# Result rows scattered to their token by GpSimd, and read back with plain loads

## The reference

```python
x = x + 0.5 * ffn(layernorm(x))      # 8 experts, 2 chosen per token
x = x + attn(layernorm(x))           # 16 heads, each token sees itself and the 8 before it
x = x + 0.5 * ffn(layernorm(x))

# ffn
scores = softmax(xt @ Wg + bg)
topk_probs, topk_idx = top_k(scores, 2)
h = gelu(einsum('nd,edh->enh', xt, W1) + b1)       # 128 -> 512, per expert
eo = einsum('enh,ehd->end', h, W2) + b2            # 512 -> 128
out = einsum('nk,nkd->nd', topk_probs, eo[topk_idx])
```

## Time and profile before

| | |
|---|---|
| median of 3 runs | 1525.34 us (1511.35 to 1526.21) |
| profiled execution | 1513.94 us, its span 1512.0 us |
| TensorE matmul busy | 1036.3 us, 69% of the span |
| VectorE busy | 760.6 us, 50% |
| ScalarE busy | 681.0 us, 45% |
| GpSimd busy | 561.6 us, 37%, of it 280.6 us in 256 scatters of x rows and 274.4 us in 256 gathers of result rows |
| mean granted TensorE clock | 0.88 |
| DMA | 95.26 MB, mean 63 GB/s |

### The profile page before, as it was taken

One profiled execution on the slowest core, in us unless ns is written; L12 is line 12 of the kernel. 1 busy time (PEld: TensorE's weight loads), 2 busy tenths in 40 slices (PEclk: granted clock), 3 DMA queues, 4 the chain that ended last, 5 costly groups with the idle time before them and its releaser, 6 DMA issues.

```text
span 1512.0 us, 24681 instructions
## 1 busy us (share of the span) xinstructions
PE 1036.3 (69%) x7729; PEld 767.0 (51%) x7729; DVE 760.6 (50%) x1344; ACT 681.0 (45%) x1395; POOL 561.6 (37%) x536
## 2 busy tenths in 40 slices
PE   3201869798787999983699208998878878788500
PEld 2200657666565478642455107746767656566400
DVE  3160434643454498449643926529945534445322
ACT  4221776675557194430044004618537655556400
POOL 1755052442545000326653454000152445442275
PEclk9999799899998999996898558999898999999855
DMA  8121132334333010000110012001112333333322
GB/s 285 48 83 54 36 82 71 78 116 109 89 81 71 13 44 22 25 15 28 32 32 21 21 35 67 15 7 29 38 56 61 88 78 92 88 82 75 107 80 71
DMA packets 151308, 95.26 MB, mean 63 GB/s; under 512 B 96370, under 2 KB 136850, under 8 KB 150164
## 3 DMA queue, kind: packets, MB, share of 16 engines
q1 hardware_dynamic: 134804, 60.10, 14.5%
q0 software_dynamic: 16384, 33.59, 8.3%
HBM read 25.46 MB, written 47.71 MB: 48 GB/s over the span
## 4 chain that ended last, share of the span: by engine, by line
PE 44%; DVE 14%; POOL 12%; issue 12%; ACT 8%; DMA 4%; another core or an unknown queue 4%; SPq 1%; ACTq 0%; POOLq 0%; DVEq 0%
PE bank L801 12%; PE bank L705 9%; PE bank L784 8%; POOL x_sorted L464 7%; POOL y_in L487 5%; PE bank L718 5%; PE bank L803 3%; PE bank L691 3%; ACT h_f L638 3%; ACT xn L523 2%; DVE h_hl L1175 2%; DMA x_sorted<-hl,slots_all 2%; PE bank L665 2%; DVE x_sb L930 2%
## 5 line engine op out<-in xcount | busy, mean ns | idle before, releaser
L464 POOL DMA_INDIRECT x_sorted<-hl,slots_all x256 | 280.6, 1096 | 515.0 <-DVE slots_all L910 352.8
L487 POOL DMA_INDIRECT y_in<-y_rows,y_row x256 | 274.4, 1072 | 426.4 <-DMA y_rows<-y_sb 194.1
L801 PE MATMUL bank<-w_hl,h_hl 128*128 x3744 | 317.2, 230 | 123.9 <-DVE h_hl L1175 59.2
L638 ACT ACTIVATE h_f<-bank,b_cols 128x256 f32<-128x256 f32 x624 | 261.3, 470 | 254.8 <-PE bank L784 163.4
L1175 DVE TENSOR_TENSOR h_hl<-h_f,h_hl 128x512 f16<-128x512 f32 x312 | 212.6, 687 | 259.8 <-ACT h_hl L644 219.7
L784 PE MATMUL bank<-xsT,w_hl 128*128 128x256 f16 x1872 | 259.2, 291 | 121.0 <-DMA xsT<-x_sorted 117.3
L801 PEld LDWEIGHTS bank<-w_hl,h_hl 128*128 128x128 f16 x3744 | 246.4, 102 | 182.2 <-issue 149.6
L784 PEld LDWEIGHTS bank<-xsT,w_hl 128*128 x1872 | 181.6, 104 | 166.6 <-issue 127.2
L644 ACT CAST h_hl<-h_f 128x512 f16<-128x512 f32 x312 | 192.8, 618 | 9.9
L718 PE MATMUL bank<-prod,ident 128*128 128x256 f32 x576 | 143.9, 411 | 40.4 <-DVE prod L1000 35.9
L718 PEld LDWEIGHTS bank<-prod,ident 128*128 128x128 f32 x576 | 117.9, 208 | 60.3 <-DVE prod L1000 39.1
(11 more groups left out here) (115 smaller groups left out, 726.1 us busy)
## 6 DMA issues: line engine op xcount, KB each, us to landing
y_rows<-y_sb SPq DMA_DIRECT2D x156, 128.0 KB
x_sb<-in_L_attn_x SPq DMA_DIRECT2D x4, 1024.0 KB, 5.6
x_sorted<-hl,slots_all POOLq DMA_INDIRECT x256
x_sorted<-no_rows SPq DMA_DIRECT2D x16, 256.0 KB, 2.1
y_in<-y_rows,y_row POOLq DMA_INDIRECT x256
out<-x_sb SPq DMA_DIRECT2D x4, 1024.0 KB
xsT<-x_sorted SPq DMA_TRANSPOSE x156
qkv<-in_L_ffn_W SPq DMA_DIRECT2D x1, 2048.0 KB, 10.4
```

The lines of the kernel that those rows point to most:

```text
L464: pool.indirect_dma_start(out=x_sorted[PART_OF[g]], out_offset=bass.IndirectOffsetOnAxis(ap=slots_all[:, at:at + 1], axis=0), in_=hl[:, ha ...
L487: pool.indirect_dma_start(out=y_in[:, j % (J // 2), k, :], out_offset=None, in_=y_rows[p], in_offset=bass.IndirectOffsetOnAxis(ap=y_row[:, ...
L638: ins = act.activation(h_f[:, u % H_BANKS, c % 2, :], bank[u % H_BANKS][:, (c % 2) * 256:(c % 2 + 1) * 256], ACT.Gelu, bias=b1_cols[:, bas ...
L801: pe.matmul(y_bank[:, half, :], h_hl[:, t.par, hs, c, mine], w_flat[:, bass.ds(at + ws * D, D)], start=(c == 0 and hs == ws == 0), stop=False)
```

## The change

Each sorted row grows from 256 to 288 16-bit values (576 bytes), and carries an id, the number of its pair (2 x token + choice), in the two values behind the 256 that the tile load takes. Since both copies of a token's row now differ, hl holds a row for each pair: it is filled by quarters of a group (Q = 4) rather than halves. Padding rows carry the id 2N, which is out of bounds. For each tile SP also loads its 256 ids (4 bytes each) into one of eight buffers tile_ids. After take_y, GpSimd writes the tile's results with two indirect DMAs of 128 rows straight to the pair's place in y_pairs, and skips ids out of bounds. SP reads a group's results back with four plain loads of 512 KB. SP's stores of results, GpSimd's gathers and the row calculation at the end of plan are gone. Tails are half as long and are cleared in both passes. The order strings are new, SP has one as well, and the last down of a part now comes before the first up of the next in all three places (begins_late).

```diff
-TAIL = 2 * SLOT_TILE
+TAIL = SLOT_TILE
+ROW = 288
+Q = 4
+JQ = J // Q
+IDS = 8
...
 POOL_ORDER = (
-    "ssssssssggggggggggsggggsssggssssgggggggggggggggg"
+    "ssssssssyyysyyyyyyyyysyyyyyyyyyysyyyyysssssyyyyyssssssssyyyyyyyyyyyyyyyyyyyyyyyyyyyyyyyyysyyyysysyyyysyysyyysss"
+    "ssssssssyyyyyyyyysyyyyysssssssyyyyyyyysyyyyyyyysyyyyssssssyyyyyyyyyyyyyyyyyyyyyyyyyyyyyyyyyyyyyyyyyyyy"
+)
...
-        self.begins_late = f > 0 and at == 0
+        self.begins_late = self.n > 0 and at == 0
...
-        hl = sb("hl", [P, 2, J // 2, 2 * D], F16)
+        hl = sb("hl", [P, 2, JQ, 2, ROW], F16)
...
+                if t.n >= IDS:
+                    sp.wait_ge(y_scattered[t.ring], (t.n - IDS) // 4 * (2 * DMA) + 2 * DMA)
+                sp.dma_start(tile_ids[:, t.n % IDS], x_sorted[t.p][bass.ds(row, SLOT_TILE), 2 * D:2 * D + 2].rearrange("(i p) c -> p i c", i=2)
+                             ).then_inc(ids_loaded[t.n % IDS], DMA)
...
+            def load_y(f, g):
+                p = PART_OF[g]
+                if g == PARTS[p][0]:
+                    for s in range(4):
+                        sp.wait_ge(y_scattered[s], 2 * DMA * len(range(s, f * NT + FIRST[p] + HT[p], 4)))
+                for c in range(C):
+                    use = (f * G + g) * C + c
+                    if use >= 2:
+                        sp.wait_ge(combined, use - 1)
+                    sp.dma_start(y_in[:, c % 2 * JC:(c % 2 + 1) * JC].rearrange("p j k d -> p (j k d)"),
+                                 y_v[g][:, c * (2 * JC * D):(c + 1) * (2 * JC * D)]).then_inc(y_loaded[c], DMA)
+                    yield
...
+            pool.memset(hl[:], 0.0).then_inc(pool_step, 1)
...
+            def scatter_y():
+                for t in ALL_TILES:
+                    pool.wait_ge(ids_loaded[t.n % IDS], (t.n // IDS + 1) * DMA)
+                    pool.wait_ge(y_ready, t.n + 1)
                     carry_waits(pool)
...
+                    for i in range(2):
+                        pool.indirect_dma_start(
+                            out=y_pairs, out_offset=bass.IndirectOffsetOnAxis(ap=tile_ids[:, t.n % IDS, i, :].bitcast(U32), axis=0),
+                            in_=y_sb[:, t.ring, i, :], in_offset=None, bounds_check=2 * N - 1, oob_is_err=False
+                        ).then_inc(y_scattered[t.ring], DMA)
                     yield
...
+            def low_halves(q, quarters):
+
+                for c in quarters:
+                    dve.wait_ge(hi_ready, Q * q + c + 1)
+                    dve.tensor_tensor(hl[:, c % 2, :, :, D:2 * D],
+                                      xn[:, c * JQ:(c + 1) * JQ, :].rearrange("p j (o d) -> p j o d", o=1).to_broadcast([P, JQ, 2, D]),
+                                      hl[:, c % 2, :, :, 0:D], ALU.subtract)
...
+                    yield from low_halves(g, (0, 1))
                     yield from route(0, g)
+                    yield from low_halves(g, (2, 3))
...
                     dve.wait_ge(y_done, t.n + 1)
                     if t.n >= 4:
-                        dve.wait_ge(y_stored[t.ring], t.n // 4 * DMA)
+                        dve.wait_ge(y_scattered[t.ring], t.n // 4 * (2 * DMA))
                     dve.tensor_copy(y_sb[:, t.ring], y_bank).then_inc(y_ready, 1)
```

222 lines of the change are left out of this document (94 added, 128 removed).

## The result

The changed kernel takes 1548.76 us (median of 4 runs, 1535.43 to 1552.59) against 1523.51 (4 runs, 1511.35 to 1526.21) of the kernel before on the same chip: a ratio of **1.0164 [1.0094, 1.0234]**, slower by 0.9 to 2.3%. The forecast was 1489 us, faster, and the range 1430 to 1550. The profiled execution took 1549.86 us, its span is 1548.1 against 1512.0: 36 us more. The medians differ by 25 us; the other 11 are there mostly because the profiled execution before was a short one of its kind. The tables of stages go by the profiled executions.

A forecast was written before the change was run, and what follows sets the result against it. It took TensorE's time per tile, slowed by GpSimd's DMAs, and its waits for scatters as the bound. Stage terms summed to a span of 1476 against 1512.0, 36 us less: median 1525 - 36 = 1489 us, range 1430 to 1550.

The forecast's parts named there:

- The end: From last copy to span's end: 40 us instead of 91, as plain loads replace gathers; a gain of 51 us.
- The last stage: Final stage of tiles, 1243 to 1421 before: 178 us becomes 39 x 4.0 + 3 + 9 = 168 us.
- The stop before tile 78: TensorE waits in the second pass for group 1's scatters; the stop stays, still over 20 us.
- Part 0's stops: First pass: TensorE stops around group 3's block of routing and 32 scatters; tile 39 starts at 426, 76 us later.
- Given back: First pass: attention turns earlier in tile order, starting at 469 as before, with 12 tiles (36 us of TensorE's work) less done.
- 467 to 844: Attention up to group 1's slots: 349 us busy plus 60 idle make 409, slots at 878, 34 late.
- Two scatters with every tile: Each tile's pair of scatters slows it: 4.0 us a tile, kept between 3.4 and 4.6, against 3.2 if free.
- 0.6 us of tile time for each of GpSimd's DMAs: Price read from tile stages of the kernel before: every GpSimd DMA beside a tile lengthens it by 0.6 us.
- The pairs cost nothing: Rival on the tiles' scatter pairs: 3.4 us a tile or less, 69 us less on 115 tiles, 1420 us; chance 0.17.
- dear: Rival: pairs cost as much as bursts, 4.6 us a tile, 69 us more on 115 tiles, 1558 us; chance 0.22.
- the stretch from 467 to 1268: Attention's start to tile 117: 409 us to group 1's slots, tile 78 at 939, then 329 us.
- The lever from part 0: First pass: tile 39 starts 76 us later, yet attention starts as before, leaving 12 tiles (36 us) for later.

The follow-up runs named there:

- e9: The changed kernel with all scatters of tile results left out (loads of results read input rows of the same size): 1430.92 us.
- e2: The changed kernel with only the first scatter of each tile, the second left out: 1446.1 us.
- e1: The changed kernel with a second PSUM bank for the result of every other tile in the stages without attention: 1543.63 us, ratio 1.0178.
- e8: The changed kernel with a tile's pair of scatters sent off later, behind VectorE's second split of the next tile: 1554.15 us.
- e12: The changed kernel with all ids of each tile's second scatter out of bounds, so that it moves no row: 1549.15 us.
- h2: h1 with two low halves of group 0 moved behind other work on VectorE: 1455.19 us, ratio 1.0118 to the kernel before.
- h3: The kernel of h2 unaltered, run once more: 1458.0 us, ratio 1.0147 to the kernel before.
- h1: The change made in the second pass alone, the first pass storing and gathering as in the kernel before: 1540.46 us, ratio 1.0058.
- b2: The kernel before without its 256 gathers, one plain load of input rows by GpSimd for each chunk instead: 1418.41 us.
- a1: The changed kernel unaltered, on a chip where the kernel before takes 1437.92 us: 1457.45 us, ratio 1.0141.
- e13: e5 without GpSimd's landing waits after bursts of row scatters, in all parts: 1547.52 us, ratio 1.0128.
- e5: The changed kernel with group 2's and 3's bursts one at a time between part 0's pairs, group 3 routed ahead of its bursts: 1529.69 us, ratio 1.0069.

## Why the prediction was wrong, by its steps

| mark | forecast | measured | late by |
|---|---|---|---|
| tile 39's first up | 426 | 432 | 6 |
| attention's first turn | 469 | 484 | 15 |
| slots of group 1 | 878 | 921.6 | 44 |
| tile 78 | 939 | 989.1 | 50 |
| tile 117 | 1268 | 1335 | 67 |
| last copy | 1436 | 1505.8 | 70 |
| span | 1476 | 1548.1 | 72 |

By the medians the miss is 60 us (1489 and 1548.76). The other 12 are there because the forecast kept the 11.4 us by which the profiled execution before was short, and that of the kernel after was not short.

**Right.** "The end": 40 us, measured 42.3. The last stage: 168 forecast, 171 measured. The stop before tile 78 stays, and group 2's attention fills part of it. Part 0's stops: the second was put at 35 to 40 us and is 48.7. The forecast's tile 39 without any price of the pairs (426 less 25 us) is e9's 401.6. GpSimd's busy time, 620 forecast, is 641.2. Attention begins 15 us later than forecast, and so not when it did.

**Wrong by its size: "Given back" and "467 to 844".** Moving tiles past the start of attention was priced at 12 x 3.0 = 36 us of TensorE's work. It is 13 tiles: 31 copies stand in 484 to 922 where 18 stood in 467 to 844. TensorE's three lines of tile matmuls, each summed by itself, take 123.3 us after and 65.1 before, so 58 us for 13 tiles, 4.5 each. With overlaps of the lines counted once it is 115.1 and 60.6: 4.2 us for each tile more, and 3.7 a tile on average. The last stage has 149.53 / 39 = 3.8. The 3.0 is that of the best rows, 32.80 us for 11 tiles at a granted clock of 1.00; here the clock is 0.91, in the last stage 0.97. The two largest lines of attention (L716, L729) take 183.1 us for 173.8, which is the 9 us forecast for group 2's windows. The base was low as well: the earlier trace rows was read as 304 us of work from 467 to 844, the trace has 309.9. Together TensorE's busy time came to 376 us instead of 349; the idle time was right (60 forecast, 62 measured). So a stretch of 409 us took 437. In e9, whose scatters are gone, the same stretch is 420 us long against some 397 forecast without the price: 23 us of error that no scatter makes. It is the largest miss among the terms of the order.

**Wrong by its size: "Two scatters with every tile".** The price of the pairs came to 115 tiles x 0.76 = 87 us; e9 shows 119. Where tiles stand alone 4.0 was near (4.18), but part 0's tiles carry bursts as well, and the middle, 78 to 117, took 343.3 for 308.4 without scatters. Of the 72 us missed, 32 are this, and the other 40 are the order's terms: 1389 forecast without the price, against e9's 1429.2 (one execution).

**Wrong in its form, and near by luck: "0.6 us of tile time for each of GpSimd's DMAs".** A price for each would make a tile with one scatter 3.8 us; e2 shows 3.24. The cost depends on whether a matmul ends within an issue, so the first scatter is nearly free and the second and third are dear. The 4.0 was picked between the half and the whole of a price that doesn't add up that way.

**Wrong in kind: the rival "The pairs cost nothing".** It was given 1420 us and a chance of 0.17, as a faster kernel. On one chip where the changed kernel was measured its premise came true for the tiles, at 3.24 us each, and the kernel was slower by 1.4%. The price of GpSimd's DMAs was read from rows of the kernel before; had it been nothing, the kernel before wouldn't have taken 1512 us either (it takes 1437 on that chip). The rival changed one side of a comparison. The rival "dear", 1558, was nearest in time, but for the wrong reason: tiles at 4.18 and not 4.6.

**The chances.** No case doubted the stretch from 467 to 1268, and 36 us of gain were less than what the errors of the order's terms turned out to be (40). The lever from part 0 (76 us, given back by attention that starts at the same time) was the place to doubt: work was moved from a stage with room on TensorE to one without.

**Still open.** What delays TensorE's signals beside GpSimd's issues, and why on some chips only; e1, e8 and e12 rule out the result bank alone, a strict hold until the pair's end, and the moved bytes, and leave the packets of a skipped scatter. How the 19 us on the other chips split by stage: no trace of the kernel before was taken there, and h2 and h3 stand for its first pass only. Whether h2 gains over h1 where the hold exists wasn't tried.

## What to carry to other kernels

A price read from the kernel before is in that kernel's own time as well: a rival that says "this costs nothing" has to take it out of both kernels before it compares them. What pays for a shorter end, here 13 tiles moved into a stage where TensorE is nearly full, is priced by the busy time of such work in such a stage (3.7 us a tile on average, 4.2 for each one more), not by its best rows (3.0). And to split a change of transport and order, leave the transport out of each kernel (e9, b2). Such a split holds where it was measured: here it gave 119, 95 and 12.5 us, and on another chip the ratio it led to expect (0.97 to 0.99) didn't come (1.014).

## What the runs showed of the hardware that I had not expected

- Results of TensorE reach VectorE and ScalarE late when GpSimd is issuing indirect DMAs: a copy starts 1.1 to 1.3 us after the matmul at the median, up to 4.6, though 11 of 47 start at once, and 0.03 us after it when GpSimd is silent. On two other chips it is 0.03 us in both cases (a1 and h3 on one, h2 on the other). The kernel before takes 1437 us on those and 1519 to 1533 on the others, the largest effect of this case.
- An indirect DMA whose 128 ids are all out of bounds takes GpSimd as long as any other: 0.98 us at the median for both kinds in e12, and the kernel's time doesn't change (1549.15). In the timeline of e12:

```profile
1450.05 0.98 POOL L503 DMA_INDIRECT y_pairs<-y_sb,tile_ids  x1 [1.91 <-issue]
...
1451.33 1.07 POOL L503 DMA_INDIRECT y_pairs<-y_sb,no_rows  x1 [0.30 <-issue]
```

- Taking out GpSimd's waits for landing between bursts of scatters gains nothing, though it shortens the two stops behind runs of them by 23 us (e13 1.0128, e5 1.0069).
